# Attention and feed-forward on one core: the coefficient of a head comes from GpSimd in the blocks of three and four key tiles too

## The reference

```
q, k: rotary positions; q scaled; causal mask
probs = softmax(q k^T)                      # 32 maps a batch
diff  = probs[:, :, 0] - lambda_full * probs[:, :, 1]
attn  = diff @ v, then an RMS norm by head, times subln_weight, @ Wo^T
x = x + attn
x = x + ffn(layernorm(x))                   # w1, w2 quantised to -1, 0, 1; gelu
```

## Time and profile before

| | |
|---|---|
| time, median of 3 runs | 4198.97 us (4195.23 to 4203.26) |
| time of the profiled execution | 4199.09 us |
| its span, first to last instruction | 4197.2 us |
| busy: PE, DVE, ACT, POOL | 83%, 76%, 69%, 42% |
| the blocks t = 2 and t = 3 of batch 3, from first exponential to first exponential | 56.29 us and 59.92 us |

### The profile page before, as it was taken

One profiled execution on the slowest core, in us unless ns is written; L12 is line 12 of the kernel. 1 busy time (PEld: TensorE's weight loads), 2 busy tenths in 40 slices (PEclk: granted clock), 3 DMA queues, 4 the chain that ended last, 5 costly groups with the idle time before them and its releaser, 6 DMA issues.

```text
span 4197.2 us, 84069 instructions
## 1 busy us (share of the span) xinstructions
PE 3491.2 (83%) x23454; PEld 2099.4 (50%) x23454; DVE 3189.3 (76%) x5170; ACT 2885.2 (69%) x6784; POOL 1776.2 (42%) x2333
## 2 busy tenths in 40 slices
PE   2688888888888888888888888888888888888886
PEld 1355554555444555455545555555545555555553
DVE  6777877778678886788767887778867778677882
ACT  1577766777667775677766777667766777667772
POOL 1244443454334543345432544334443444334543
PEclk6899999999999999999999999999999999999999
DMA  3101011000011001000011010111001010110000
GB/s 133 38 19 34 20 34 34 29 20 26 29 34 34 18 28 38 29 25 29 21 34 34 20 34 16 36 31 34 20 30 34 22 31 20 35 34 29 20 28 14
DMA packets 146840, 128.57 MB, mean 31 GB/s; under 512 B 66608, under 2 KB 117680, under 8 KB 145840
## 3 DMA queue, kind: packets, MB, share of 16 engines
q1 hardware_dynamic: 146352, 122.79, 9.1%
HBM read 67.61 MB, written 55.12 MB: 29 GB/s over the span
## 4 chain that ended last, share of the span: by engine, by line
PE 42%; DVE 22%; issue 19%; ACT 12%; POOL 2%; ACTq 1%; DVEq 1%; DMA 1%; SPq 0%; POOLq 0%
PE M L864 9%; PE F L936 7%; DVE NM L707 7%; PE SP_ L879 6%; PE M L914 5%; PE F L953 5%; PE DP L891 4%; DVE NM L715 4%; DVE E L734 3%; ACT E L579 3%; ACT DT L591 2%; PE M L858 2%; ACT L579 2%; ACT L596 1%; PE DX L891 1%
## 5 line engine op out<-in xcount | busy, mean ns | idle before, releaser
L579 ACT ACTIVATE E<-SP_,NM 128x256 f32<-128x256 f32 (+7 forms) x2048 | 1523.5, 744 | 922.6 <-DVE NM L715 527.2
L707 DVE TENSOR_REDUCE NM<-SP_ 128x1 f32<-128x896 f32 (+3 forms) x1024 | 1031.7, 1018 | 291.9 <-PE SP_ L880 286.5
L879 PE MATMUL SP_<-KST,QST 96*128 96x512 f16 (+3 forms) x3072 | 828.2, 341 | 372.1 <-ACT E L579 316.0
L734 DVE SCALAR_TENSOR_TENSOR E<-E,CC 128x512 f32<-128x512 f32 (+7 forms) x1024 | 941.4, 919 | 49.3 <-POOL CC L494 30.0
L891 PE MATMUL DP<-ident,E 128*128 128x128 f32 x3328 | 569.6, 286 | 85.7 <-DVE E L734 76.2
L879 PEld LDWEIGHTS SP_<-KST,QST 96*128 96x128 f16 x3072 | 274.4, 101 | 712.4 <-ACT E L579 487.1
L591 ACT ACTIVATE DT<-DP 128x512 f32<-128x512 f32 (+3 forms) x1024 | 525.7, 513 | 123.2 <-PE DP L891 117.0
L491 POOL TENSOR_TENSOR RP<-SUM,minus 128x1 f32<-128x1 f32 x512 | 292.5, 571 | 722.5 <-ACT E L579 708.2
L715 DVE TENSOR_REDUCE NM<-SP_ 128x2 f32<-128x1024 f32 (+3 forms) x512 | 419.2, 819 | 198.9 <-PE SP_ L880 188.9
L864 PE MATMUL M<-WQKV,WT 128*128 128x512 f32 x1040 | 546.0, 618 | 17.9 <-DVE TOK L775 11.0
L936 PE MATMUL F<-X2H,W1Q 128*128 128x256 f16 x2048 | 499.6, 282 | 31.3 <-DVE SQ L803 16.6
(11 more groups left out here) (96 smaller groups left out, 4847.3 us busy)
## 6 DMA issues: line engine op xcount, KB each, us to landing
scratch<-SPL SPq DMA_DIRECT2D x65, 576.0 KB, 2.8
QST<-scratch SPq DMA_DIRECT2D x390, 64.0 KB, 2.4
X<-in_x SPq DMA_DIRECT2D x66, 256.0 KB, 2.8
out<-SQ SPq DMA_DIRECT2D x64, 256.0 KB, 2.0
KST<-scratch SPq DMA_DIRECT2D x390, 32.0 KB, 1.9
DT<-in_w2T SPq DMA_DIRECT2D x1, 4096.0 KB, 25.9
KST<-in_w1T SPq DMA_DIRECT2D x2, 1024.0 KB, 10.6
WQKV<-in_wqT SPq DMA_DIRECT2D x1, 1024.0 KB, 6.6
```

The costliest lines, as they stand in the source:

```text
L579: act.activation(dst, score_out(i, 2 * n + k, w), ACT.Exp, bias=NM[:, (2 * u + k) % 8:(2 * u + k) % 8 + 1], scale=1.0, accum_out=SUM[:, i ...
L707: nc.vector.tensor_reduce(NM[:, m:m + 1], score_out(i, 2 * n + k, P * (i + 1)), AX.X, ALU.max, negate=True).then_inc(max_ready, 1)
L734: nc.vector.scalar_tensor_tensor(out=E1[:, u % 4, 0:w], in0=E2[:, u % 2, 0:w], scalar=CC[:, u % 4:u % 4 + 1], in1=E1[:, u % 4, 0:w], op0=A ...
L879: pe.matmul(SP_[:, k[a // 512], 0:n], q, KST[0:ROWS, a // P:(a + n) // P, kk, :], start=True, stop=not last)
```

## The change

For t = 2 and t = 3 the coefficient moves from DVE to GpSimd: the limit 4 becomes `RATIO_TILE = 2`. The counts of the semaphores follow (`ratio_ready` and `d_chain` go up by 1 instead of 2, with totals a batch to fit). Nothing else is moved. It concerns 2 blocks of 16 heads in 8 batches, 256 heads. Two lines are added at the top, so a line of the changed kernel has a number higher by 2 (L491 becomes L493, L734 becomes L736).

```diff
--- before.py
+++ after.py
@@ -107,6 +107,8 @@
 N_PV = pg(TILES - 1, 1, 1) + 1
 N_E = NQ * TILES
 N_U = H * TILES
+RATIO_TILE = 2
+RATIO_HEADS = N_U - H * RATIO_TILE
 
 
 LN1_STATS, LN1_ROWS, LN1_TURN = 1, 3, 6
@@ -484,7 +486,7 @@
 
                 u = i * H + n
                 gu = b * N_U + u
-                gp = b * (N_U // 2) + u - N_U // 2
+                gp = b * RATIO_HEADS + u - H * RATIO_TILE
                 col = 8 * (n // 8) + 4 * (n % 2) + (n % 8) // 2
                 c = slice(u % 4, u % 4 + 1)
                 hold(pool, exp_done, 2 * gu + 2)
@@ -492,12 +494,12 @@
                 hold(pool, d_ready, gu - 3)
                 hold(pool, inverse_out, gp + 1)
                 pool.tensor_scalar(CC[:, c], RP[:, c], SUM[:, i % 2, 0, col:col + 1], neglam[:, 0:1], ALU.mult,
-                                   ALU.mult).then_inc(ratio_ready, 2)
+                                   ALU.mult).then_inc(ratio_ready, 1)
 
             def pool_work(T):
                 for hs in range(HS_TILE):
                     old = T.before(hs // 2 - 1)
-                    if hs % 2 == 0 and old and old[1] >= 4:
+                    if hs % 2 == 0 and old and old[1] >= RATIO_TILE:
                         ratio(*old)
                     if T.attend:
                         if hs == LN1_STATS:
@@ -721,16 +723,16 @@
                 gu = b * N_U + u
                 w = P * (i + 1)
                 col = 8 * (n // 8) + 4 * (n % 2) + (n % 8) // 2
-                if i >= 4:
-                    after(dve, ratio_ready, b * N_U + 2 * u - N_U + 2)
+                if i >= RATIO_TILE:
+                    after(dve, ratio_ready, b * RATIO_HEADS + u - H * RATIO_TILE + 1)
                 else:
-                    gd = b * 2 * N_U + 4 * u
+                    gd = b * (2 * H * RATIO_TILE) + 2 * u
                     after(dve, exp_done, 2 * gu + 2)
-                    nc.vector.reciprocal(R2[:, u % 4:u % 4 + 1], SUM[:, i % 2, 1, col:col + 1]).then_inc(d_chain, 2)
+                    nc.vector.reciprocal(R2[:, u % 4:u % 4 + 1], SUM[:, i % 2, 1, col:col + 1]).then_inc(d_chain, 1)
+                    after(dve, d_chain, gd + 1)
+                    nc.vector.tensor_scalar(CC[:, u % 4:u % 4 + 1], R2[:, u % 4:u % 4 + 1], SUM[:, i % 2, 0, col:col + 1],
+                                            neglam[:, 0:1], ALU.mult, ALU.mult).then_inc(d_chain, 1)
                     after(dve, d_chain, gd + 2)
-                    nc.vector.tensor_scalar(CC[:, u % 4:u % 4 + 1], R2[:, u % 4:u % 4 + 1], SUM[:, i % 2, 0, col:col + 1],
-                                            neglam[:, 0:1], ALU.mult, ALU.mult).then_inc(d_chain, 2)
-                    after(dve, d_chain, gd + 4)
                 nc.vector.scalar_tensor_tensor(out=E1[:, u % 4, 0:w], in0=E2[:, u % 2, 0:w], scalar=CC[:, u % 4:u % 4 + 1],
                                                in1=E1[:, u % 4, 0:w], op0=ALU.mult, op1=ALU.add).then_inc(d_ready, 1)
```

## The result

The changed kernel takes 4234.6 us (median of 4 runs, 4230.7 to 4238.73) against 4197.1 us (4194.09 to 4203.26) of the kernel before: ratio 1.0086, 95% interval 1.0071 to 1.0102, so slower by some 36 us. The profiled execution took 4233.09 us, its span is 4231.2 us.

What follows compares the result with a forecast made beforehand. No engine alone bounds the kernel; engines hand over to each other, and GpSimd's queue order decides. 7 x 2.3 (blocks of three) + 8 x 2.65 (blocks of four) - 1 (batch 0) = 36.3 us: 4235 us, range 4196 to 4266.

Steps and rivals of the forecast that it cites:

- batch 0: Block of three tiles in the batch without HH and HL or b2 sums: -1 us, at most -2.7.
- GpSimd's queue in the block of four: Heads 7 to 11: coefficients queue with other work, 16.67 us or more; the chain feels +3.2 us, block net +2.65.
- the tail: Rest of the block of four after head 11: one place on the chain, head 13, gains 0.55 us.
- Block of three: Heads 0 to 5 queue behind GpSimd's work: head 5 late by 2.4 us (1.8 to 4.1), block net +2.3.
- Head 8: Block of three: its coefficient stands behind the sum with b2, yet its combination starts 0.4 us earlier.
- The lower bound that I gave this block: Block of three: least net loss +1.5 us, from head 5 late by 1.8 and a further gain.
- Head 15: End of the block of three: coefficient behind the sum with b2, combination +0.86 us late, next block's layer norm queued behind.
- the first half of the block of four as 0: Block of four from its start to the exponential of head 7: no loss counted, 0 us.
- the semaphores' steps as neutral: Stepping by 1 instead of 2 was given no effect; the 114 ns before CC counted as DVE's wait.
- The relief: Rival: DVE's relief wins in blocks of three and four, at most 4.4 us a batch, 35 us, 4164; chance 0.14.
- A cancelling of the two: Rival: delays half taken up by slack, 1.5 + 1.5 us lost, 5 x 0.55 gained, 4199; chance 0.10.
- Dearer than forecast: Rival: combinations and GpSimd's work stretch each other, to 18.89 and 20.00 us; 4268 and a little over; chance 0.10.

Runs made afterwards that it cites:

- only4: Changed kernel with coefficients on GpSimd in the block of four key tiles, not in that of three; 4203.06 us, 1.0013 to the kernel before.
- inc1: Kernel before with only the semaphore steps changed, 1 instead of 2, coefficients left where they were; 4181.95 us, 0.9958 to the kernel before.
- h15: Changed kernel with the coefficient of head 15 of the block of three tiles on DVE again; 4219.41 us, 1.0053 to the kernel before.
- move2: Changed kernel with d_chain stepping by 2 again where DVE still makes the coefficient; 4241.47 us, 1.0104 to the kernel before.
- nocoef: Steps of 1, coefficients of the blocks of three and four tiles left out altogether; 4153.54 us, 0.9882 to the kernel before.
- nohl_after: Changed kernel with HL left out of GpSimd's work (set to zero once); 4166.95 us, 0.9925 to the kernel before.
- nohl_inc1: inc1 with HL left out of GpSimd's work (set to zero once); 4143.28 us, 0.9864 to the kernel before.
- sel: Steps of 1, below five tiles GpSimd coefficients only for heads where it is free and DVE comes late; 4158.23 us, 0.9902 to the kernel before.

## Why the prediction was right, and where only its sum was

**The time.** 4235 was forecast, 4234.6 measured. That close a hit is luck in good part: the blocks of four cost 15.9 us more than I said, and everything else gave 17.7 us back. The row of the blocks of three hides two more misses, which also cancel: batch 0 is +2.7 and not -1, batches 1 to 7 are +11.9 and not +16.1. By the profiles of before and after, over all 8 batches:

| | forecast | measured |
|---|---|---|
| blocks of three tiles | +15.1 | +14.6 |
| blocks of four tiles | +21.2 | +37.1 |
| everything else | 0 | -17.7 |
| sum | +36.3 | +34.0 |

**GpSimd's queue in the block of four: right.** From the exponential of head 7 to the coefficient of head 11 I summed 16.67 to 18.9 us; it was 17.07. Another window of GpSimd, from between the CC of head 7 and the sum behind it to the CC of head 11, shows 14.41 of 15.90 us busy:

```profile
1779.25:1795.15 15.90, 14.41 (x22) 0.89 0.09 38
```

The chain was to feel +3.2 and felt +2.84; the tail was to gain 0.55 and gained 0.67. The block of four in only4, where head 15 comes in time, is +2.65 against the kernel before, the number forecast, and +2.4 against inc1 (62.74 and 60.30). Inside it the three stretches are +0.57, +2.74 and -0.67, so the exact sum is a chance there too, while the stretch that the prediction was about came within 0.5 us. TensorE's clock is not a rival here: it falls to 0.50 between 1783.5 and 1786.9 in the changed kernel, but GpSimd has no gap there and its stretch has the same length in batches where the clock doesn't fall.

**Block of three: right in kind and size.** VectorE's timeline, combinations of heads 5 and 8:

```profile
1710.38 1.60 DVE L736 SCALAR_TENSOR_TENSOR E<-E,CC 128x384 f32<-128x384 f32 x1 [0.52 <-POOL CC L496]
...
1721.06 0.95 DVE L736 SCALAR_TENSOR_TENSOR E<-E,CC 128x384 f32<-128x384 f32 x1 [0.93 <-POOL CC L496]
```

GpSimd's stretch from the exponential of head 0, at 1691.14, to the CC of head 5, at 1710.35, takes 19.21 us with no gap over 0.22; 18.5 to 20.8 was the forecast. The granted clock is 0.50 for 13.7 us in this block, 6.8 in the kernel before, but with GpSimd's queue unbroken that can't be what holds head 5. Measured from the block's start head 5 is 25.57 - 22.97 = 2.60 us late (2.4 forecast). Head 8 is 36.25 - 33.74 = 2.51 late, so it gained 0.09 and not 0.4. From there to the end 0.8 us came back, 0.55 was forecast. (The lower bound that I gave this block, +1.5, doesn't follow from its own terms: 1.8 - 0.4 - 0.55 + 0.86, less a further 0.55, is 1.2.) Head 15 starts 1.28 us behind the block's end instead of 0.45: +0.83, forecast +0.86.

**The step that failed: the first half of the block of four as 0.** The +0.86 of head 15 was entered as a cost of the block of three, with a remark on the layer norm behind it, and not followed further. In the changed kernel DVE's maximum of head 1 comes 3.29 us into the block instead of 2.22 (+1.07); the clock's stretch at 0.50 then makes +2.97 of it at the maximum of head 3, at 1754.28 (11.47 into the block, 8.50 in the kernel before, whose row is below). Some 0.5 is regained, and the power over 16 columns (3.37 us) holds the coefficient of head 5, for which DVE waits 1.32 us at 1768.60. Together +3.69.

```profile
1741.86 1.22 DVE L715 TENSOR_REDUCE NM<-SP_ 128x2 f32<-128x1024 f32 x1 [0.83 <-PE SP_ L880]
```

only4, where head 15 isn't late, has a block of 62.74 us, and h15 brings back 2.42 us of the mean of 3.14: head 15 as the source of three quarters is shown. In h15 the idle time of TensorE at this place is 1.26 us, and the maximum of head 3 is never later than 8.58 us into the block. That the fall of the clock comes from the 2.01 us of idle TensorE is not shown: no run changed this idle time alone, batch 2 has the same 2.01 us without a fall in the next 30 us, and inc1, which moves nothing and has 1.20 us there, has the same kind of fall in batches 5 and 7 (maximum of head 3 after 10.30 us instead of 8.68).

**The second step that failed: the semaphores' steps as neutral.** They are worth 17.4 us alone and 6.9 us in the changed kernel (inc1, move2). I had read the 114 ns as a price of the dependence. They hide part of the move's price. The blocks of one key tile are 6.6 us shorter in batches 1 to 7; the steps explain about half of it (49.83 to 49.31 us for the shortest such block). The other half is not theirs, since move2, with steps of 2 in these blocks, is 5.5 us shorter there: the kernel before has more blocks of up to 51.64 us among them, and these have the clock at 0.50 for 5.4 to 9.1 us instead of 3.1 to 3.4. The move itself, 42 us on equal steps, is dearer than my 36.3.

**Batch 0.** Forecast -1 for its block of three, measured 50.07 against 47.40, +2.7. Without HH and HL GpSimd is free, and DVE still waits for it, by 0.17 to 1.52 us at ten heads, because DVE comes sooner than 1.1 us behind the exponential. The clock is 0.84 instead of 0.90 there too; inc1, which moves nothing, has 0.85 and 48.96, so some 1.6 of the +2.7 need not be the move's.

**Busy times.** GpSimd's 35.12 and 34.89 us stand against 35.6 and 33.7. DVE's fell by 3.07 and 4.08 us, not by 6.8: 16 combinations are longer by 0.14 us each, 2.2 us. The rest isn't assigned to rows here.

**The rivals.** The relief exists (28 us, nocoef), but DVE got none of it where it waits. A cancelling of the two is excluded by the interval. "Dearer than forecast" named stretching of both engines: it is there, 2.2 us a block on DVE, but little of it reaches the time. In nohl_after the combinations of the block of three are as stretched (820 ns against 699 in nohl_inc1), and the block is only 0.21 us longer.

## What to carry to other kernels

Before work is moved to an engine with idle time, write that engine's stream down beside the moments at which the results are wanted: here the order in the queue and the latency (1.1 us against 0.54) decided, not the busy share. Moving 10 of 32 heads (and 8 in shorter blocks), each where its consumer was late anyway, gained 24 us where moving all 32 lost 53. Look at what an edit does to the instructions besides its purpose, the steps of a semaphore included, and test the two apart: here they had opposite signs. Follow a delay at the end of a block into the next one.

## What was not expected of the hardware

- **An instruction that steps its semaphore by 2 has its wait ahead of it as a separate instruction.** 114 ns from reciprocal to CC with steps of 2, 40 ns with steps of 1, same operations and data (512 each). The Trainium skill, "Trainium Kernel Development and Optimization", section "Key Constraints", says that compute semaphores go up by 1; it gives no price, and here a step of 2 works and costs 74 ns between these two instructions.
- **Combination and GpSimd's next work start together now.** The CC that releases DVE also frees GpSimd. At 1760.01 a combination of 128x512 beside the square at 1759.93 takes 1.51 us, at 1755.57 with GpSimd idle 0.75 us. VectorE's timeline:

```profile
1755.57 0.75 DVE L736 SCALAR_TENSOR_TENSOR E<-E,CC 128x512 f32<-128x512 f32 x1
...
1760.01 1.51 DVE L736 SCALAR_TENSOR_TENSOR E<-E,CC 128x512 f32<-128x512 f32 x1
```

  The mean rose from 840 to 979 ns in the changed kernel and only to 871 in sel; without HL it rose from 809 to 961. The Trainium skill, "SBUF — State Buffer", section "Who interferes with whom", has such a pair exclude each other; the trace agrees in kind: the combination is longer by 0.76 us, where waiting for the end of the square would have made it 0.96.
- **The same power took 2.91 us before and 3.37 us in the changed kernel** (128x16, GpSimd), at that place beside DVE's work; what stretched it was not tried. The row of the kernel before:

```profile
1751.71 2.91 POOL L520 TENSOR_TENSOR RST<-VE,nhalf 128x16 f32<-128x16 f32 x1 [4.14 <-DVE VE L783]
```
